# Gated cross-attention with a mixture of experts: half of the projections placed between the score matmuls

## The chip, the core and the metric

The kernel runs on one core of a Trainium2 chip. The metric is the device time of one execution in microseconds (us). The core has TensorE (matmuls into PSUM, which has 8 banks), VectorE, ScalarE, GpSimd (which the code calls pool) and SyncE (sp), whose queue only issues DMAs. Each engine runs its own instructions strictly in the order written, and waits on semaphores for the others.

## What is computed

B = 8 batches of S = 512 tokens with D = 512 channels; attention has 16 heads of 32 channels.

```python
def ref_attention(query, key, value):
    Q, K, V = proj(query, Wq, bq), proj(key, Wk, bk), proj(value, Wv, bv)
    scores = jnp.einsum('bhqd,bhkd->bhqk', Q, K) / SCALE
    attn = jax.nn.softmax(scores, axis=-1)
    out = jnp.einsum('bhqk,bhkd->bhqd', attn, V)
    out = out.transpose(0, 2, 1, 3).reshape(B, S, D)
    return out @ Wo.T + bo
...
x = x + jnp.tanh(g_xattn[0]) * ref_attention(_layernorm(x), ctx_1024, ctx_1024)
x = x + jnp.tanh(g_ffn[0]) * ref_ffn(_layernorm(x))   # 8 experts, top 2, capacity 1.2
```

## The kernel before

**Stages.** Attention comes first, batch by batch, then the routing, then the experts. The change lies in attention alone. Products are kept exact enough by splitting each operand into a high and a low half of 16 bits, so a projection of one 128x512 tile is 12 matmuls: 4 tiles of the contraction, 3 pairs of halves.

**A batch on TensorE** (the function batch under block.tensor). First come the 8 query and key products, qk 0 to 7 in the order q0, k0, q1, k1 and so on (96 matmuls, line 1158). ScalarE copies each out of PSUM twice (qk32 and the high half in qks), GpSimd subtracts for the low half (line 515, "the split"), and SyncE's queue sends both halves to DRAM and back, stacked three high, into stk (stack_heads, one write and three reads for each product). Heads 4m to 4m + 3 need products 2m and 2m + 1.

Then come SLOTS = 23 slots. Slot s has up to four scores matmuls (line 1236), whose only use is the maximum of each row, which VectorE takes from PSUM (line 831, banks 0 and 1 in turn). Every fourth slot the maxima of four heads are split, transposed (mhl, mrow) and sent into row 96 of stk. Six slots later, less_maxima (line 1246) computes the same scores transposed, less the maxima, for unit u = s - 6, in two halves (banks 2, 3 and 4, 5). ScalarE takes their exponentials (line 709, pt), and slot s has with_values and with_ones for unit s - 7 (lines 1255 and 1262), which add up in banks 6 and 7 over the four units of a group. At a group's end ScalarE copies both banks (osum), VectorE takes four reciprocals and multiplies (t32, line 874), ScalarE makes the high half aT (line 721) and GpSimd the low one. Group 1's t32 falls in slot 17, group 2's in slot 20. After the slots TensorE does the output product (48 matmuls, line 1335), banks 2, 4, 0 and 1.

**Between the pairs of scores** lie other pieces: the value product v (48 matmuls, line 1273) in slots 0, 1, 3 and 4 to 5, as halves of six matmuls, and the router of the batch before: transposes of x2n in slot 2, parts and logits in slot 4. In slots 16 to 22 the next batch's normalised x and ctx are transposed, one 128x512 tile in each slot from 16 to 21 and two in slot 22, in banks 1 and 0 in turn (inputs_transposed). VectorE makes their high half (line 807), then their low half (line 810), which frees the bank:

```python
if not (isinstance(b, int) and b == 0):
    ps, _ = filled(dve, act_use, ("actT", n, kt), b)
    v.tensor_scalar(actT[:, n, 0, kt, :], ps, (1.0, SX)[n], None, ALU.mult).then_inc(act_hi, 1)
```

**Order on the other engines** is the order of the code too. In one slot VectorE does: mhl (in every fourth), four maxima, input halves, reciprocals, t32, statistics for the next layer norm (LN_SLOT, slots 6 to 9). ScalarE does: copies of v and of the router, two exponentials, osum, aT. Behind the slots VectorE adds the residual, takes statistics, normalises to x2n with deviations from GpSimd (inverse_deviation), and splits x2n in x2hl.

**Banks.** A class Banks counts the uses of each bank; claim waits on TensorE until the use before has been read, filled waits on a reader until TensorE has written, and copied waits until a use has been read.

Of the kernel before, what the change touches and what calls it, by code (L numbers as in the profile page):

```python
# [45 lines left out]
LN_SLOT = LAG_B  # L46
V_HALF = ((0, 0), (1, 1), (3, 3), (4, 5))
V_SLOT = [last for _, last in V_HALF]
X2T_SLOT, LG_SLOT = 2, 4
GROUP_END = [LAG_C + 4 * g + 3 for g in range(NG)]  # L50
GROUP_NORM = [t + 3 if t < UNITS else min(t + 2, SLOTS) for t in GROUP_END]

# [31 lines left out]
def layer_kernel(nc, x, ctx_in, g_x, g_f, Wq, bq, Wk, bk, Wv, bv, Wo, bo, Wr, br, W1, b1, W2, b2, out):  # L84
# [9 lines left out]
    with stack:  # L94
# [175 lines left out]
        bank_full = [sem(f"bank_full{i}") for i in range(6 + 1)]  # L270
        bank_read = [sem(f"bank_read{i}") for i in range(6 + 1)]
# [103 lines left out]
        def _(sp):  # L375
# [35 lines left out]
            def batch(b, first, last):  # L411
# [12 lines left out]
                for i in range(NQ):  # L424
                    stack_heads(sp, b, i)
                for g in range(NG):
# [5 lines left out]
                    if g == 0:  # L432
                        if not first:
# [47 lines left out]
        def _(pool):  # L481
# [159 lines left out]
        def _(act):  # L641
# [8 lines left out]
            s.activation(bias[:, 8:12], ps[:, 8:12], ACT.Copy, scale=SA).then_inc(bias_ready, 1)  # L650

            def inputs_hi(n, kt):

                ps, _ = filled(act, pre, ("actT", n, kt))
                s.activation(actT[:, n, 0, kt, :], ps, ACT.Copy, scale=(1.0, SX)[n]).then_inc(act_hi, 1)

            for n in range(4):
# [3 lines left out]
                if n < 2:  # L661
                    for kt in range(KT):
                        inputs_hi(n, kt)
            act.wait_ge(bias_ready, 2)

            def router_copy(where, b, slot):
# [6 lines left out]
                def logits():  # L673
                    ps, read = filled(act, where, "lg_parts", b)
                    s.activation(lg_parts[:, :], ps, ACT.Copy).then_inc(read, 1)
                    ps, read = filled(act, where, "lg", b)
# [814 lines left out]
```

## Time and profile before

| | |
|---|---|
| time, median of 3 runs | 1959.96 us (1959.57 to 1960.15) |
| profiled execution, own time | 1961.34 us |
| its span, first to last instruction | 1959.6 us |
| mean granted clock of TensorE | 0.964 |
| busy share of the span: TensorE, VectorE, ScalarE, GpSimd | 91%, 60%, 40%, 25% |
| attention in the span | about 0 to 960 us |
| one batch of it (first scores to first scores) | 402.26 to 519.6 us |
| a middle slot | 3.94 us |

In the profile PE is TensorE, DVE VectorE, ACT ScalarE, POOL GpSimd and SPq the queue of SyncE. An L number is a line of the kernel. A row names what an instruction writes, an arrow, and what it reads; "x6" behind it is a count of instructions merged in the row. The brackets say how long the engine had been idle before it and which engine's instruction ended that. A granted clock of 1.00 is TensorE at full rate.

### The profile page before, as it was taken

What the parts mean: (1) busy time and instruction counts of PE and PEld (TensorE: products, weight loads), DVE (VectorE), ACT (ScalarE), POOL (GpSimd) and SP (SyncE); (2) the same over time, 40 slices, a digit from 0 to 9 for tenths busy, and PEclk for the clock granted to TensorE, in tenths of its full rate; (3) what the DMA queues carried; (4) which work ended last, traced back from release to release, by engine and by line L of the source; (5) the groups of instructions that cost most, each with busy time, mean ns of one, the idle gap of its engine ahead of it and who ended that gap; (6) DMA issues with size and microseconds to landing.
All of it is one profiled execution on the core that took longest, in us unless ns stands there. A gap on an engine that the chain in (4) does not pass through costs nothing.

```text
span 1959.6 us, 30460 instructions
## 1 busy us (share of the span) xinstructions
PE 1788.7 (91%) x10822; PEld 919.9 (47%) x10822; DVE 1167.3 (60%) x2163; ACT 780.9 (40%) x1012; POOL 484.3 (25%) x451
## 2 busy tenths in 40 slices
PE   7999999999999999999811799999999999999996
PEld 4334242332424334242200566667676767666664
DVE  5777868777686777867587453635354443534330
ACT  5443634445354443634430342515161524334240
POOL 2313333232333313331141121221212211112101
PEclk9999999999999999999955899999999999999998
DMA  6214123150322414023130153433334342424311
GB/s 223 84 44 151 45 94 100 48 166 22 127 66 82 133 43 153 19 73 100 37 141 1 48 141 72 149 77 121 102 96 124 82 140 50 154 66 138 70 45 25
DMA packets 138205, 178.97 MB, mean 91 GB/s; under 512 B 45492, under 2 KB 86592, under 8 KB 134056
## 3 DMA queue, kind: packets, MB, share of 16 engines
q1 hardware_dynamic: 97192, 157.85, 24.7%
q0 software_dynamic: 40960, 20.41, 6.0%
q8 instruction: 33, 0.54, 0.1%
q14 instruction: 20, 0.16, 0.0%
HBM read 134.08 MB, written 43.63 MB: 91 GB/s over the span
## 4 chain that ended last, share of the span: by engine, by line
PE 83%; DVE 9%; ACT 3%; issue 2%; DMA 2%; SPq 1%; POOL 1%; DVEq 0%; ACTq 0%; POOLq 0%
PE psum L1445 21%; PE psum L1422 20%; PE psum L1158 7%; PE psum L1255 6%; PE psum L1262 6%; PE psum L1246 5%; PE psum L1236 5%; PE psum L1335 4%; PE psum L1273 4%; DVE mx L831 2%; PE psum L1163 2%; ACT osum L717 1%; DMA qk_rows<-qks 1%; PE psum L1398 1%; DVE cmp L980 1%
## 5 line engine op out<-in xcount | busy, mean ns | idle before, releaser
L1445 PE MATMUL psum<-w,hT 128*123 128x512 f16 x1920 | 420.3, 379 | 0.0
L831 DVE TENSOR_REDUCE mx<-psum 128x1 f32<-128x512 f32 x512 | 328.5, 684 | 153.4 <-PE psum L1236 152.6
L1422 PE MATMUL psum<-xgT,w 128*128 128x308 f16 (+1 forms) x3072 | 411.3, 294 | 0.6 <-DVE xgT L1089 0.6
L1422 PEld LDWEIGHTS psum<-xgT,w 128*128 128x128 f16 x3072 | 298.4, 97 | 109.7 <-DVE xgT L1089 0.8
L1445 PEld LDWEIGHTS psum<-w,hT 128*123 128x123 f16 x1920 | 257.9, 135 | 148.8
L709 ACT ACTIVATE pt<-psum 128x1024 f32<-128x1024 f32 x256 | 259.3, 1022 | 171.0 <-PE psum L1246 171.0
L759 ACT ACTIVATE h<-psum,b1c 128x308 f32<-128x308 f32 (+1 forms) x256 | 118.1, 512 | 379.4 <-PE psum L1422 379.0
L1107 DVE TENSOR_TENSOR hT<-h,hT 128x615 f16<-128x615 f32 x128 | 102.6, 801 | 212.2 <-ACT hT L762 212.1
L629 POOL DMA_INDIRECT out_dram<-y,idx_now x40 | 98.9, 2473 | 499.6 <-DVE y L1142 273.9
L1236 PE MATMUL psum<-stk 96*128 96x512 f16 x512 | 171.7, 384 | 20.0 <-DVE mx L831 18.9
L1158 PE MATMUL psum<-actT,wT 128*128 128x512 f16 x768 | 168.6, 381 | 2.0 <-DVE wT L818 2.0
L743 ACT ACTIVATE w<-stage 128x2048 f16<-128x2048 f32 x64 | 121.7, 1902 | 101.4 <-DMA stage<-in_L_ffn_W_dram 101.4
L1084 DVE SCALAR_TENSOR_TENSOR w<-stage,w 128x512 f16<-128x512 f32 x240 | 156.7, 685 | 0.3 <-issue 0.3
L1246 PE MATMUL psum<-stk 98*128 98x512 f16 x512 | 154.1, 382 | 0.9 <-DMA stk<-mrow 0.9
L1255 PE MATMUL psum<-pt,v 128*32 128x512 f32 x1024 | 137.1, 608 | 5.3 <-ACT osum L717 5.0
L1262 PE MATMUL psum<-pt,ones 128*32 128x512 f32 x1024 | 136.2, 604 | 0.0
L1236 PEld LDWEIGHTS psum<-stk 96*128 96x128 f16 x512 | 43.8, 98 | 192.6 <-DVE mx L831 144.8
L1139 DVE SCALAR_TENSOR_TENSOR y<-psum,b2b 123x512 f32<-123x512 f32 x40 | 27.7, 692 | 178.8 <-PE psum L1445 178.8
L1158 PEld LDWEIGHTS psum<-actT,wT 128*128 128x128 f16 x768 | 75.4, 98 | 93.7 <-issue 4.3
L583 POOL DMA_INDIRECT xg<-x_split,idx_new x40 | 62.0, 1551 | 221.7 <-issue 178.9
L515 POOL TENSOR_TENSOR qks<-qk,qks 128x512 f16<-128x512 f32 x64 | 82.6, 1297 | 76.8 <-ACT qks L692 75.7
L535 POOL TENSOR_SCALAR a<-t,bias 128x512 f32<-128x512 f32 x32 | 22.3, 696 | 315.9 <-DVE t L874 315.9
(181 smaller groups left out, 1682.1 us busy)
## 6 DMA issues: line engine op xcount, KB each, us to landing
stage<-in_L_ffn_W_dram SPq DMA_DIRECT2D x64, 1024.0 KB, 5.0
stk<-qk_rows SPq DMA_DIRECT2D x192, 128.0 KB, 2.5
qk_rows<-qks SPq DMA_DIRECT2D x64, 256.0 KB, 2.6
xin<-in_x_dram SPq DMA_DIRECT2D x8, 1024.0 KB, 5.1
cin<-in_ctx_dram SPq DMA_DIRECT2D x8, 1024.0 KB, 5.1
xres<-in_x_dram SPq DMA_DIRECT2D x8, 1024.0 KB, 5.8
out_dram<-xres SPq DMA_DIRECT2D x32, 256.0 KB, 2.1
x_split<-x2hl SPq DMA_DIRECT2D x32, 256.0 KB, 2.3
```

What stands on the lines that cost most here:

```text
L709: s.activation(pt[:, (2 * u + hf) % 4, :, :], psum[:, bank:bank + 2, :], ACT.Exp, scale=1.0 / (math.sqrt(HD) * SQ * SQ)).then_inc(read, 1)
L743: s.activation(dst, stage[:, i % 2, :], ACT.Copy, scale=SW).then_inc(chunk_hi, 1)
L759: s.activation(h32[:, m % 4, c0:c1], psum[:, (2 * m + ch) % 4, 0:c1 - c0], ACT.Silu, scale=1.0 / (SX * SW), bias=b1c[:, e, m:m + 1]).then_ ...
L831: v.reduce_max(mx[:, KT * t + qt:KT * t + qt + 1], ps, AX.X).then_inc(read, 1)
L1084: v.scalar_tensor_tensor(part[1], stage[:, i % 2, cols], SW, part[0], ALU.mult, ALU.subtract).then_inc(chunk_split, 1)
L1158: last = t_.matmul(dst, lhsT, rhs, start=(i == 0), stop=(i == len(pairs) - 1))
L1236: t_.matmul(dst, stk[0:96, 0, s, qt * P:(qt + 1) * P], stk[0:96, 1, s, :], start=True, stop=True).then_inc(full, 1)
L1246: last = t_.matmul(psum[:, 2 + 2 * hf + j, :], stk[0:98, 1, h, kt * P:(kt + 1) * P], stk[0:98, 0, h, :], start=True, stop=True)
L1255: t_.matmul(psum[32 * j:32 * j + 32, 6, :], v32[:, kt, HD * h:HD * h + HD], pt[:, (2 * u + j // 2) % 4, j % 2, :], start=(kt == 0), stop=( ...
L1262: last = t_.matmul(psum[32 * j:32 * j + 32, 7, :], ones32[:, :], pt[:, (2 * u + j // 2) % 4, j % 2, :], start=(kt == 0), stop=(kt == KT - 1))
L1422: mm = t_.matmul(psum[:, (2 * m + ch) % 4, 0:c1 - c0], w1[:, wp, kt, m * P:(m + 1) * P], xgT[:, xp, kt, c0:c1], start=(kt == 0 and (wp, xp ...
L1445: mm = t_.matmul(psum[0:CP, Y_BANK[c], :], hT[:, hp, k, c * CP:(c + 1) * CP], w2[:, wp, k, :], start=(k == 0 and (hp, wp) == (0, 0)), stop ...
```

## The change

- Only four query and key products and two value tiles are done ahead of the slots. Products 4 to 7 move to slots 0, 1, 3 and 4, value tiles 2 and 3 to slots 5 and 6. Each is cut in two halves of six matmuls, one behind each pair of scores; the transposes of slot 2 are cut likewise. parts stays in slot 4, logits goes to slot 5. Banks 3, 5, 6 and 7 take some of these tiles.
- VectorE takes two maxima ahead of mhl and two behind. Its layer-norm statistics move from slots 6 to 9 to slots 1 to 4.
- The high half of the transposed inputs moves from VectorE to ScalarE, behind the two exponentials of the slot. The low half stays on VectorE, and it waits for the high one.
- GpSimd makes the second layer norm's deviations of the batch before ahead of splits 0 and 2 of the next batch, not at the end of the batch.
- SyncE's queue stacks products 0 to 5, sends the maxima of group 0, stacks 6 and 7, and stores the rows of the batch before behind group 1.

```diff
@@ -43,12 +43,23 @@
 UNITS = 4 * NG
 LAG_B, LAG_C = 6, 7
 SLOTS = UNITS + LAG_C
-LN_SLOT = LAG_B
-V_HALF = ((0, 0), (1, 1), (3, 3), (4, 5))
-V_SLOT = [last for _, last in V_HALF]
-X2T_SLOT, LG_SLOT = 2, 4
+LN_SLOT = 1
+QK_FIRST, QK_SLOT = 4, (0, 1, 3, 4)
+V_FIRST, V_SLOT = 2, (5, 6)
+X2T_SLOT, PARTS_SLOT, LG_SLOT = 2, 4, 5
+STORE_GROUP = 1
 GROUP_END = [LAG_C + 4 * g + 3 for g in range(NG)]
 GROUP_NORM = [t + 3 if t < UNITS else min(t + 2, SLOTS) for t in GROUP_END]
+def later_qk(s):
+    return [QK_FIRST + j for j, slot in enumerate(QK_SLOT) if slot == s]
+def later_v(s):
...
@@ -218,21 +229,25 @@
         pre = banks.close(1)
         def batch_banks(last):
-            for i in range(NQ):
-                banks.add(("qk", i), (2, 4, 0, 1, 0, 1, 2, 4)[i])
+            for i in range(QK_FIRST):
+                banks.add(("qk", i), (2, 4, 0, 1)[i])
+            for tt in range(V_FIRST):
+                banks.add(("v", tt), (3, 5)[tt])
             for s in range(SLOTS):
                 for qt in range(2):
                     if s < UNITS:
                         banks.add(("S", s, qt), qt)
+                for i in later_qk(s):
+                    banks.add(("qk", i), (2, 4, 2, 4)[i - QK_FIRST])
                 if s == X2T_SLOT:
                     for kt in range(KT):
-                        banks.add(("x2T", kt), (2, 4)[kt % 2])
-                for tt in range(KT):
-                    if s == V_HALF[tt][0]:
-                        banks.add(("v", tt), (2, 4, 2, 2)[tt])
+                        banks.add(("x2T", kt), (6, 7, 3, 5)[kt])
+                if s == PARTS_SLOT:
+                    banks.add("lg_parts", 6)
+                for tt in later_v(s):
+                    banks.add(("v", tt), (3, 6)[tt - V_FIRST])
                 if s == LG_SLOT:
-                    banks.add("lg_parts", 4)
-                    banks.add("lg", 4)
+                    banks.add("lg", 7)
                 if not last:
...
@@ -421,7 +436,7 @@
                 sp.wait_ge(norm_done, NG * b)
                 settle(sp)
-                for i in range(NQ):
+                for i in range(QK_FIRST + 2):
...
@@ -430,6 +445,9 @@
                     for a in range(4):
                         sp.dma_start(rows[:, :, a, :], mrow[32 * a:32 * a + 32, g, :]).then_inc(mrow_in[g], 16)
                     if g == 0:
+                        for i in range(QK_FIRST + 2, NQ):
+                            stack_heads(sp, b, i)
+                    if g == STORE_GROUP:
                         if not first:
                             store_rows(b)
...
@@ -504,11 +522,14 @@
             for tt in range(KT):
                 inverse_deviation(0, tt, tt)
-            def batch(b, last):
+            def batch(b, first, last):
                 heads_stacked(pool, b)
                 for i, (which, m) in enumerate(QK_ORDER):
+                    if i in (0, 2) and not first:
+                        for tt in (i, i + 1):
+                            inverse_deviation(1, tt, KT * b + (tt - KT))
                     n = "qk".index(which)
                     pool.wait_ge(qk32_ready, NQ * b + i + 1)
...
-                for tt in range(KT):
-                    inverse_deviation(1, tt, KT * b + tt)
-            batch(0, False)
+            batch(0, True, False)
             with pool.Fori(1, B - 1) as b:
-                batch(b, False)
-            batch(B - 1, True)
+                batch(b, False, False)
+            batch(B - 1, False, True)
+            for tt in range(KT):
+                inverse_deviation(1, tt, KT * (B - 1) + tt)
...
+            s.activation(bias[:, 8:12], ps[:, 8:12], ACT.Copy, scale=SA).then_inc(read, 1)
+            def inputs_hi(b, n, kt):
+                ps, _ = filled(act, act_use, ("actT", n, kt), b)
                 s.activation(actT[:, n, 0, kt, :], ps, ACT.Copy, scale=(1.0, SX)[n]).then_inc(act_hi, 1)
...
                     ps, read = filled(act, where, "lg", b)
                     settle(act)
                     s.activation(lg[:, slot, :], ps[:, 0:KT * E], ACT.Copy).then_inc(read, 1)
-                return rows, logits
+                return rows, parts, logits
             def batch(b, last):
-                rows, logits = router_copy(use, b, b)
-                heads_stacked(act, b)
...
@@ -691,12 +714,25 @@
                                  bias=bias[:, 4 * n + m:4 * n + m + 1]).then_inc(qk32_ready, 1)
                     s.activation(qks[:, n, 0, m, :], ps, ACT.Identity, scale=SQ / (SX * SW),
                                  bias=bias[:, 4 * n + m:4 * n + m + 1]).then_inc(read, 1)
+                def values(tt):
+                    ps, read = filled(act, use, ("v", tt), b)
+                    s.activation(v32[:, tt, :], ps, ACT.Copy, scale=1.0 / (SX * SW)).then_inc(read, 1)
+                heads_stacked(act, b)
+                for i in range(QK_FIRST):
+                    queries_keys(i)
+                for tt in range(V_FIRST):
+                    values(tt)
                 for t in range(SLOTS + 1):
-                    if t in V_SLOT:
-                        ps, read = filled(act, use, ("v", V_SLOT.index(t)), b)
-                        s.activation(v32[:, V_SLOT.index(t), :], ps, ACT.Copy, scale=1.0 / (SX * SW)).then_inc(read, 1)
+                    for i in later_qk(t):
+                        queries_keys(i)
                     if t == X2T_SLOT:
                         rows()
+                    if t == PARTS_SLOT:
+                        parts()
+                    for tt in later_v(t):
+                        values(tt)
                     if t == LG_SLOT:
                         logits()
                     u = t - LAG_B
...
@@ -708,6 +744,9 @@
                             _, read = filled(act, use, ("ST", u, hf), b)
                             s.activation(pt[:, (2 * u + hf) % 4, :, :], psum[:, bank:bank + 2, :], ACT.Exp,
                                          scale=1.0 / (math.sqrt(HD) * SQ * SQ)).then_inc(read, 1)
+                    if not last:
+                        for i in act_tiles(t):
+                            inputs_hi(b + 1, i // KT, i % KT)
                     if t in GROUP_END[:-1]:
                         gr = GROUP_END.index(t)
...
@@ -802,9 +842,6 @@
             def inputs_split(b, n, kt):
-                if not (isinstance(b, int) and b == 0):
-                    ps, _ = filled(dve, act_use, ("actT", n, kt), b)
-                    v.tensor_scalar(actT[:, n, 0, kt, :], ps, (1.0, SX)[n], None, ALU.mult).then_inc(act_hi, 1)
                 dve.wait_ge(act_hi, 2 * KT * b + (KT * n + kt + 1))
                 ps, read = read_by_last(act_use, ("actT", n, kt), b)
                 v.scalar_tensor_tensor(actT[:, n, 1, kt, :], ps, (1.0, SX)[n], actT[:, n, 0, kt, :],
...
@@ -843,6 +880,7 @@
                         v.reciprocal(osum[:, 1, i * P:(i + 1) * P], sums[:, i * P:(i + 1) * P]).then_inc(rinv_done, 1)
                 for t in range(SLOTS + 1):
+                    maxima(t, (0, 1))
                     if t % 4 == 0 and 4 <= t <= UNITS:
                         g = t // 4 - 1
                         for qt in (2, 3):
@@ -856,7 +894,7 @@
                         dve.wait_ge(mrow_in[g], 64 * b)
                         v.transpose(mrow[:, g, :], mhl[:, g, :]).then_inc(mrow_ready, 1)
-                    maxima(t, range(KT))
+                    maxima(t, (2, 3))
                     if not last:
                         for i in act_tiles(t):
                             inputs_split(b + 1, i // KT, i % KT)
...
@@ -1220,14 +1258,22 @@
             def batch(b, last_batch, first=False):
                 rows, parts, logits = router(use, b, KT * b)
-                for i, (which, m) in enumerate(QK_ORDER):
+                def queries_keys(i, halves=range(2)):
+                    which, m = QK_ORDER[i]
                     n = "qk".index(which)
                     if m == 0:
                         for kt in range(KT):
                             copied(pe, act_use, ("actT", n, kt), b)
-                    dst, full = claim(pe, use, ("qk", i), b)
-                    product(dst, [(wT[:, n, wp, kt, m * P:(m + 1) * P], actT[:, n, xp, kt, :])
-                                  for kt in range(KT) for wp, xp in PARTS]).then_inc(full, 1)
+                    if 0 in halves:
+                        claim(pe, use, ("qk", i), b)
+                    bank, _ = use(("qk", i), b)
+                    for kt in [2 * half + j for half in halves for j in range(2)]:
+                        for wp, xp in PARTS:
+                            last = t_.matmul(psum[:, bank, :], wT[:, n, wp, kt, m * P:(m + 1) * P], actT[:, n, xp, kt, :],
+                                             start=(kt == 0 and (wp, xp) == (0, 0)),
+                                             stop=(kt == KT - 1 and (wp, xp) == (1, 0)))
+                    if 1 in halves:
+                        last.then_inc(bank_full[bank], 1)
...
@@ -1263,19 +1309,36 @@
                                              pt[:, (2 * u + j // 2) % 4, j % 2, :], start=(kt == 0), stop=(kt == KT - 1))
                         last.then_inc(pv_done, 1)
-                def values(tt, half):
-                    if half == 0:
+                def values(tt, halves=range(2)):
+                    if 0 in halves:
                         claim(pe, use, ("v", tt), b)
                     bank, _ = use(("v", tt), b)
-                    for kt in (2 * half, 2 * half + 1):
+                    for kt in [2 * half + j for half in halves for j in range(2)]:
                         for xp, wp in PARTS:
                             last = t_.matmul(psum[:, bank, :], actT[:, 1, xp, kt, tt * P:(tt + 1) * P], wT[:, 2, wp, kt, :],
                                              start=(kt == 0 and (xp, wp) == (0, 0)),
                                              stop=(kt == KT - 1 and (xp, wp) == (1, 0)))
-                    if half == 1:
+                    if 1 in halves:
                         last.then_inc(bank_full[bank], 1)
+                def filling(s, half):
+                    for i in later_qk(s):
+                        queries_keys(i, (half,))
+                    if s == X2T_SLOT:
+                        rows((2 * half, 2 * half + 1))
+                    if (s, half) == (PARTS_SLOT, 1):
+                        parts()
+                    for tt in later_v(s):
+                        values(tt, (half,))
+                    if (s, half) == (LG_SLOT, 1):
+                        logits()
+                for i in range(QK_FIRST):
+                    queries_keys(i)
+                for tt in range(V_FIRST):
+                    values(tt)
                 if first:
                     pe.wait_ge(k_ones, 1)
                 for s in range(SLOTS):
...
@@ -1284,14 +1347,12 @@
                         pe.wait_ge(stk_in[s // 4], 96 * b + 96)
                     scores(s, 0)
                     scores(s, 1)
-                    if s == X2T_SLOT:
-                        rows()
-                    for tt in range(KT):
-                        if s in V_HALF[tt]:
-                            values(tt, V_HALF[tt].index(s))
-                    if s == LG_SLOT:
-                        parts()
+                    filling(s, 0)
                     u = s - LAG_B
+                    if u == 0:
+                        copied(pe, use, ("v", 2), b)
+                        copied(pe, use, ("x2T", 3), b)
                     if 0 <= u < UNITS and u % 4 == 0:
                         pe.wait_ge(mrow_in[u // 4], 64 * b + 64)
                     less_maxima(u, 0)
@@ -1306,6 +1367,8 @@
                             if v_ == 0:
                                 pe.wait_ge(norm_done, NG * b)
+                                copied(pe, use, ("v", 3), b)
+                                copied(pe, use, "lg", b)
                             else:
                                 pe.wait_ge(osum_ready, (NG - 1) * b + v_ // 4)
                         for hf in range(2):
@@ -1317,12 +1380,8 @@
                     scores(s, 2)
                     less_maxima(u, 1)
                     scores(s, 3)
-                    for tt in range(KT):
-                        if V_HALF[tt] == (s, s):
-                            values(tt, 1)
-                    if s == LG_SLOT:
-                        logits()
                     with_ones(s - LAG_C)
+                    filling(s, 1)
                 for gs in (range(KT - 1), range(KT - 1, KT)):
                     for tt in range(KT):
                         if gs[0] == 0:
```

## Rows read from the trace of the kernel before

**Rows 1.** TensorE's waits in one batch: who waited for whom, us, times, longest
```profile
PE psum L1236 <- DVE mx L831: 2.4, 6, 0.6
PE psum L1255 <- ACT osum L717: 0.6, 3, 0.3
PE psum L1216 <- ACT t L675: 0.3, 1, 0.3
PE psum L1273 <- ACT v L697: 0.3, 1, 0.3
PE psum L1163 <- ACT x2nT L671: 0.2, 1, 0.2
```

**Rows 2.** Timeline of TensorE, slots 19 and 22: start, us, what
```profile
357.54 0.61 PE L1246 MATMUL psum<-stk 98*128 98x512 f16 x2
...
358.75 1.06 PE L1255 MATMUL psum<-pt,v 128*32 128x512 f32 x8 [0.17 <-ACT osum L717]
...
368.29 1.09 PE L1163 MATMUL psum<-ident,cin 128*128 128x128 f32 x8
```

**Rows 3.** Timeline of ScalarE, slots 17, 18 and 21
```profile
353.20 1.02 ACT L709 ACTIVATE pt<-psum 128x1024 f32<-128x1024 f32 x1 [1.01 <-PE psum L1246]
354.64 0.72 ACT L721 ACTIVATE aT<-t,bias 128x512 f16<-128x512 f32 x1 [0.42 <-DVE t L874]
355.27 1.00 ACT L709 ACTIVATE pt<-psum 128x1024 f32<-128x1024 f32 x1
...
366.83 1.92 ACT L709 ACTIVATE pt<-psum 128x1024 f32<-128x1024 f32 x2
```

**Rows 4.** Timeline of VectorE, slots 17 and 20
```profile
352.33 0.69 DVE L810 SCALAR_TENSOR_TENSOR actT<-psum,actT 128x512 f16<-128x512 f32 x1
352.94 0.94 DVE L843 RECIPROCAL osum<-osum 128x128 f32<-128x128 f32 x1
353.92 0.69 DVE L874 TENSOR_TENSOR t<-osum 128x512 f32<-128x512 f32 x1
...
363.69 1.75 DVE L843 RECIPROCAL osum<-osum 128x128 f32<-128x128 f32 x2
```

**Rows 5.** Timeline of TensorE, projections and slots 0 to 3
```profile
381.54 20.88 PE L1158 MATMUL psum<-actT,wT 128*128 128x512 f16 x96
402.26 0.60 PE L1236 MATMUL psum<-stk 96*128 96x512 f16 x2
...
403.99 0.60 PE L1236 MATMUL psum<-stk 96*128 96x512 f16 x2
...
411.88 0.60 PE L1236 MATMUL psum<-stk 96*128 96x512 f16 x2
413.05 0.39 PE L1236 MATMUL psum<-stk 96*128 96x512 f16 x1 [0.57 <-DVE mx L831]
413.65 0.39 PE L1236 MATMUL psum<-stk 96*128 96x512 f16 x1 [0.21 <-DVE mx L831]
```

**Rows 6.** Timeline of VectorE, slots 2, 6 and 7
```profile
412.30 2.48 DVE L831 TENSOR_REDUCE mx<-psum 128x1 f32<-128x512 f32 x4 [1.42 <-PE psum L1236]
...
427.74 0.69 DVE L785 BATCH_NORM_STATS2 stats<-xin 128x6 f32<-128x512 f32 x1
...
428.68 2.73 DVE L831 TENSOR_REDUCE mx<-psum 128x1 f32<-128x512 f32 x4
```

**Rows 7.** Timeline of VectorE, the end of a batch: casts for x2hl
```profile
388.62 1.38 DVE L894 CAST x2hl<-x2n 128x512 f16<-128x512 f32 x1
...
393.50 0.42 DVE L894 CAST x2hl<-x2n 128x512 f16<-128x512 f32 x1
```

**Rows 8.** Timeline of ScalarE, a copy of v
```profile
306.46 0.60 ACT L697 ACTIVATE v<-psum 128x512 f32<-128x512 f32 x1 [1.38 <-PE psum L1273]
```

**Rows 9.** Timeline of TensorE, the first projections of batch 0
```profile
27.96 22.40 PE L1158 MATMUL psum<-actT,wT 128*128 128x512 f16 x96 [2.00 <-DVE wT L818]
```

**Rows 10.** Busy us by engine, then granted clock, just behind that wait
```profile
28.00:30.00 2.00, 2.00 (x5) 0.65 (x6) 0.59 (x1) 0.00 (x0) 0.00 (x0) 0.50 0.50 111
```

More of the change, by code:

```diff
@@ L45 @@
 SLOTS = UNITS + LAG_C
-LN_SLOT = LAG_B
-V_HALF = ((0, 0), (1, 1), (3, 3), (4, 5))
-V_SLOT = [last for _, last in V_HALF]
-X2T_SLOT, LG_SLOT = 2, 4
+LN_SLOT = 1
[3 more added lines that the diff above has]
+STORE_GROUP = 1
 GROUP_END = [LAG_C + 4 * g + 3 for g in range(NG)]
 GROUP_NORM = [t + 3 if t < UNITS else min(t + 2, SLOTS) for t in GROUP_END]
+def later_qk(s):
+    return [QK_FIRST + j for j, slot in enumerate(QK_SLOT) if slot == s]
+def later_v(s):
+    return [V_FIRST + j for j, slot in enumerate(V_SLOT) if slot == s]
 def act_tiles(s):
@@ L268, in act_use @@
             return pre(key) if isinstance(b, int) and b == 0 else use_loop(key, b, back=1)
-        bank_full = [sem(f"bank_full{i}") for i in range(6 + 1)]
-        bank_read = [sem(f"bank_read{i}") for i in range(6 + 1)]
+        bank_full = [sem(f"bank_full{i}") for i in range(8)]
+        bank_read = [sem(f"bank_read{i}") for i in range(8)]
         def claim(pe, where, key, b=0):
@@ L662, in _ @@
                     for kt in range(KT):
-                        inputs_hi(n, kt)
-            act.wait_ge(bias_ready, 2)
+                        inputs_hi(0, n, kt)
+            act.wait_ge(bias_ready, 1)
+            copied(act, pre, "bias")
             def router_copy(where, b, slot):
@@ L671, in rows, with parts, logits @@
                         s.activation(x2nT[:, kt, :], ps, ACT.Copy).then_inc(read, 1)
-                def logits():
+                def parts():
                     ps, read = filled(act, where, "lg_parts", b)
                     s.activation(lg_parts[:, :], ps, ACT.Copy).then_inc(read, 1)
+                def logits():
                     ps, read = filled(act, where, "lg", b)
@@ L678, in logits, with queries_keys @@
                     s.activation(lg[:, slot, :], ps[:, 0:KT * E], ACT.Copy).then_inc(read, 1)
-                return rows, logits
+                return rows, parts, logits
             def batch(b, last):
-                rows, logits = router_copy(use, b, b)
-                heads_stacked(act, b)
-                for i, (which, m) in enumerate(QK_ORDER):
+                rows, parts, logits = router_copy(use, b, b)
+                def queries_keys(i):
+                    which, m = QK_ORDER[i]
                     n = "qk".index(which)
@@ L726, in _ @@
             batch(B - 1, True)
-            rows, logits = router_copy(post, 0, B)
+            rows, parts, logits = router_copy(post, 0, B)
             rows()
+            parts()
             logits()
@@ L1193, in router, with rows @@
             def router(where, b, n):
-                def rows():
+                def rows(kts=range(KT)):
                     pe.wait_ge(x2n_ready, n)
-                    for kt in range(KT):
+                    for kt in kts:
                         dst, full = claim(pe, where, ("x2T", kt), b)
@@ L1222, in batch @@
                 rows, parts, logits = router(use, b, KT * b)
-                for i, (which, m) in enumerate(QK_ORDER):
+                def queries_keys(i, halves=range(2)):
+                    which, m = QK_ORDER[i]
                     n = "qk".index(which)
@@ L1275, in values @@
                                              stop=(kt == KT - 1 and (xp, wp) == (1, 0)))
-                    if half == 1:
+                    if 1 in halves:
                         last.then_inc(bank_full[bank], 1)
+                def filling(s, half):
[4 more added lines that the diff above has]
+                    if (s, half) == (PARTS_SLOT, 1):
+                        parts()
+                    for tt in later_v(s):
[6 more added lines that the diff above has]
+                    values(tt)
                 if first:
```

3 lines of the change are left out of this document (removed).

## Prediction

> **What bounds the kernel now.** I read the busy shares by stage first: attention takes the first 960 us of the span, about 117.3 us for each of 8 batches, and the change touches nothing behind it. Then the waits of one whole batch, slots 0 to 22 and the products around them [rows 1]: TensorE idles 3.8 us of 117.3, so it is the bound in every slot, and no reordering can give back more than 3.8 x 8 = 30 us, 1.6%. Of the 2.4 us on VectorE, 1.8 lie in the early slots (0.57 and 0.21 behind slot 2, the same behind slot 5, 0.26 behind slot 6) and 0.55 in slot 12. Last I read the timelines of TensorE, VectorE and ScalarE side by side, early and late in the batch, to see which engine is only just on time. That is the larger question: in slots 16 to 22 ScalarE waits for VectorE's t32 and the exponentials behind it are only just early enough [rows 2 to 4].
>
> **Early slots: what the change gives.** A batch's projections are 96 + 48 matmuls at 0.216 us, before and after; nothing is saved but waits. The rhythm: VectorE starts a maximum 0.42 us after its scores (411.88 to 412.30), the next follows 0.62 later (2.48 for 4), and the bank is free 0.75 after the start (413.05, and 413.65 for the second) [rows 5, 6]. Pairs 1.73 us apart (402.26 to 403.99, six matmuls between) never wait. With halves between all pairs the five early waits on VectorE go (1.82), and so do the three on ScalarE's copies (0.3, 0.3, 0.2), as the copied banks now change and parts and logits lie a slot apart: 2.56 us a batch, **-20.5 us** for 8. In slot 12 the first two maxima now go ahead of the mhl operations, 0.49 us earlier, which leaves 0.13 of 0.55: **-3.4 us**.
>
> **What the early part costs.** (a) POOL now makes two of the four inverse deviations only behind splits 0 and 1. VectorE needs them for x2n, and its casts for x2hl (0.42 us alone, 1.38 while GpSimd works on its splits from 388.3 on [rows 7]) end at about 398.5 in place of 396.5. Scores start 24 matmuls earlier, 397.1 in place of 402.3. So the first maxima start 1.0 late, and the next two scores wait 0.42 and 0.38: 0.8 us in 7 batches, **+5.6** (0 if the casts meet no split, 1.9 a batch if all do). (b) The statistics of the next layer norm, 0.94 us each (427.74 to 428.68 [rows 6]), move from slots of 3.94 us to slots 1 to 4 of 3.0 to 3.5, where maxima take 2.5. Walked through pair by pair: waits of 0.14 and 0.40 in slot 2, 0.22 in slot 3, 0.08 in slot 4: 0.84 in 7 batches, **+5.9** (0 to 1.5 a batch). (c) v3 moves to slot 6. Its second half is TensorE's last work of that slot, and ScalarE's in-order queue has its copy ahead of both exponentials of unit 0. Let X be the end of the half: the copy starts X+0.19 and takes 0.60, as now [rows 8]; the exponential starts X+0.70, ends X+1.72, and less_maxima of unit 1, which writes the bank that it reads, starts X+1.78 in place of X+0.43: 1.35. The second exponential ends X+2.64 and with_values starts X+2.70 in place of X+2.31: 0.39. 1.74 us in 8 batches, **+13.9** (0 if the bank were free, 2.6 if nothing overlapped).
>
> The heads' DMA chain shortens with the scores: the two deviations moved let split 0 end at 387.1 in place of 389.7, so that the third stk transfer lands at about 396.5, TensorE arriving at 397.1. I cost it at nothing; without those 0.6 us it is 0 to 1 a batch. SP has mrow of group 0 behind six stackings, ready some 4 us ahead of slot 6. Storing the rows and xres move one group later; xres lands near 447, GpSimd's bias ends at 452, and its first a32 is due at 457: nothing.
>
> The Trainium skill ("SBUF — State Buffer", section Who interferes with whom) says that VectorE's two-port and two-input forms and GpSimd lock each other out for a whole instruction. The cast of 1.38 against 0.42 agrees; by that rule moving splits away from the tail speaks for this change, by the deviations against it, and (a) lies between its bounds above.
>
> **Late slots: what the moved high halves cost.** Now VectorE makes high and low half of each transposed tile as soon as TensorE is done. After, ScalarE makes the high one, behind both exponentials of its slot, and VectorE's low half waits there, ahead of its reciprocals and t32. I walk one batch [rows 2 to 4], slot 17 onwards:
> - exponential (11,1) starts 353.20; the next ScalarE step is 0.92 later, so high half 1 runs 354.12 to 354.72. VectorE's low half starts 354.75 (now 352.33), the reciprocal 0.61 later, t32 0.98 later at 356.34 (353.92), aT 0.72 later at 357.06 (354.64), exponential (12,0) 0.63 later at 357.69 (355.27). It is 2.42 late; it ends 358.71.
> - less_maxima of unit 13 needs its bank: 358.77 in place of 357.54, **1.23**.
> - exponential (12,1) 358.61, high half 2 359.53, osum 360.12 to 361.14 (a 128x1024 copy, 1.02 as an exponential). with_values of unit 12 starts 361.20 in place of 358.75. TensorE is **2.45** late.
> - Slot 20 starts 363.73. Exponential (14,1) 366.40, high half 4 367.32, low half 367.95, two reciprocals 368.56, t32 1.79 later at 370.35, aT 371.07, exponentials 371.70 and 372.62, high half 5 373.54, low half 374.17 to 374.86.
> - Slot 22 has tiles 6 and 7, and tile 7 needs the bank of tile 5. It starts 374.92; due at 368.29 + 0.51 + 2.45 = 371.25. **3.67**.
> Sum 6.12 us. Behind it all moves along: VectorE's four last reciprocals start 5.9 later, TensorE reaches group 3 of the output product 6.1 later. Seven batches have it: **+42.8** (bounds: 0.6 a batch, if only osum were later by a copy; 8 a batch, if t32 waited for each high half in full).
>
> **The clock.** At 28 us TensorE had stood still for 2.00 us, and its granted clock in the 2 us that followed was 0.50, the lower of its levels, 1.2 GHz of 2.4; 96 matmuls took 22.40 us where 20.88 is normal [rows 5, 9, 10]. I take 1.5 us for a fall. The stall of 3.67 in slot 22 is longer: 7 x 1.5 = 10.5. Stalls of 1.23 + 1.22 in slots 18 to 19 and 1.35 + 0.39 in slot 7 are near it: half of 15 x 1.5, 11. **+22** (0 to 33). The Trainium skill ("TensorE: Matmul & The Clock Gate", Part 1) states that an idle array falls to half its clock and must earn it back. The row agrees with that; without such falls the sum would be 22 less.
>
> **The sum.** -20.5 - 3.4 + 5.6 + 5.9 + 13.9 + 42.8 + 22 = +66 us, against the profiled execution's span of 1959.6 and own time of 1961.3. The median shown is 1.4 below that time, so 1960 + 66 = **2026 us**.
>
> **Rivals.**
> - *ScalarE's queue as above, forecast*: 2026, its own range 2004 (clock never falls) to 2045 (falls at every stall, and the stk chain 1 us late). Chance 0.66.
> - *The late stalls are smaller.* Should t32 not wait for low halves, only osum is late, by one copy of 0.6: 4.2 in place of 42.8, and no clock fall there: 1960 + 5.7, with slot 7 falling 0 to 12: 1966 to 1978; half way to the forecast 1990. For it: ScalarE is busy for 40% of the span only. Against it: VectorE's order, low half, reciprocal, t32, is plain [rows 4]. Chance 0.18.
> - *Faster: ScalarE's idle time absorbs v3 and the high halves.* Decisive is whether exponential (12,0) is less than 1.19 us late, the room between its end (356.3) and the 357.54 at which its bank is wanted, and (0,0) likewise. Then -20.5 - 3.4 + 11.5 = -12: 1948. The walk has 2.42 against 1.19. Chance 0.05.
> - *VectorE and the clock worse*: falls cascade, each making the next group's t32 later: above 2045. Chance 0.08.
> - *It does nothing*: the same matmuls, stalls that only change place: 1960. Chance 0.03.
>
> Within 0.2% (4 us) is about what a measurement can't tell from no change. Faster by more: 0.05. Same: 0.03. Slower: 0.92. Leaving out the ends of the rivals: 1990 to 2046.
>
> **What would show it.** In the changed profile: the early waits for mx after slots 2 and 5 gone, a wait of about 1.3 us of the first less_maxima of slot 7, a wait of about 1.2 at slot 19 for ScalarE's pt, then osum 1.2, and one of 3 to 4 us of the transposes of cin for VectorE's actT; t32 of group 2 some 5 us later against the transposes; granted clock below 1.00 in attention windows. I am wrong if ScalarE's exponentials stay 0.65 us behind less_maxima in slots 18 to 21, if the batch is under 119 us, or if the first scores wait for stk.

## The result, and the profile after

| | before | changed |
|---|---|---|
| time, median | 1959.76 us (1958.46 to 1960.15, 4 runs) | 2015.82 us (2011.98 to 2021.84, 4 runs) |
| profiled execution, own time | 1961.34 us | 2011.98 us |
| its span | 1959.6 us | 2010.2 us |
| mean granted clock | 0.964 | 0.958 |

The changed kernel takes 1.0289 times as long, 95% interval 1.0267 to 1.0312. The forecast was 2026 us with 1990 to 2046. The spread of the changed kernel, 10 us, is much wider than the 1.7 us of the kernel before. The clock is the likely cause: the mean granted clock of the four runs was 0.958, 0.957, 0.955 and 0.953 at 2011.98, 2012.99, 2018.64 and 2021.84 us, and 0.005 of 2015 us is 10 us.

TensorE's waits in the changed kernel, over the whole of attention: who waited for whom, us, times, longest. They answer to [rows 1], which are of one batch.

```profile
PE psum L1201 <- DVE actT L847: 24.4, 7, 3.5
PE psum L1292 <- ACT pt L745: 17.3, 15, 1.2
PE psum L1301 <- ACT osum L756: 12.7, 24, 1.3
PE psum L1282 <- DVE mx L868: 11.0, 22, 1.8
...
PE psum L1301 <- ACT pt L745: 3.5, 9, 0.4
```

The kernel before, over its attention:

```profile
PE psum L1236 <- DVE mx L831: 18.9, 48, 0.6
```

Two of the changed kernel's rows did not exist before: the transposes wait for VectorE's low half (7 batches), and less_maxima for an exponential (8 batches in slot 7, 7 in slot 19). with_values waited for an exponential once before, 0.3 us, and now nine times. The waits for the copies x2nT, t and v are gone, and those for mx fell from 18.9 to 11.0 us.

The timeline of TensorE in the batch that begins at 289.21 us. The first three rows are at slot 7, the next at slot 12, then slots 19 and 22; they answer to [rows 2].

```profile
316.81 0.60 PE L1282 MATMUL psum<-stk 96*128 96x512 f16 x2
318.58 0.61 PE L1292 MATMUL psum<-stk 98*128 98x512 f16 x2 [1.17 <-ACT pt L745]
319.59 1.06 PE L1301 MATMUL psum<-pt,v 128*32 128x512 f32 x8 [0.40 <-ACT pt L745]
...
344.48 0.39 PE L1282 MATMUL psum<-stk 96*128 96x512 f16 x1 [1.75 <-DVE mx L868]
...
366.56 1.06 PE L1308 MATMUL psum<-pt,ones 128*32 128x512 f32 x8
368.77 0.60 PE L1292 MATMUL psum<-stk 98*128 98x512 f16 x2 [1.14 <-ACT pt L745]
369.21 0.60 PE L1201 MATMUL psum<-ident,xn 128*128 128x128 f32 x4
371.08 1.40 PE L1301 MATMUL psum<-pt,v 128*32 128x512 f32 x8 [1.27 <-ACT osum L756]
...
382.21 0.66 PE L1201 MATMUL psum<-ident,cin 128*128 128x128 f32 x4
386.35 1.12 PE L1201 MATMUL psum<-ident,cin 128*128 128x128 f32 x4 [3.49 <-DVE actT L847]
```

The reader sees four stalls. Each is priced by start times, as in the prediction. Slot 7: less_maxima was due 0.43 us after the scores at 316.81, at 317.24, and started at 318.58, 1.34 late (forecast 1.35); with_values was due 0.53 behind it and came 0.48 late (0.39). Slot 19: due at 367.56, 1.00 behind with_ones, started 1.21 late (1.23), and then with_values at 371.08 for 369.74, 1.34 late; in the kernel before it was itself 0.24 late there (358.75 for 358.51 in [rows 2]), so 1.10 is new (1.22). Slot 22: tile 7 due 0.51 behind tile 6, at 382.72, started 3.63 late (3.67). Only slot 12 was not forecast.

ScalarE and VectorE in slots 17 to 22 of the same batch, which answer to [rows 3, 4]:

```profile
363.22 1.02 ACT L745 ACTIVATE pt<-psum 128x1024 f32<-128x1024 f32 x1 [1.01 <-PE psum L1292]
364.14 0.59 ACT L675 ACTIVATE actT<-psum 128x512 f16<-128x512 f32 x1
367.08 0.72 ACT L760 ACTIVATE aT<-t,bias 128x512 f16<-128x512 f32 x1 [2.35 <-DVE t L912]
367.71 1.92 ACT L745 ACTIVATE pt<-psum 128x1024 f32<-128x1024 f32 x2
369.52 0.60 ACT L675 ACTIVATE actT<-psum 128x512 f16<-128x512 f32 x1
369.99 1.03 ACT L756 ACTIVATE osum<-psum 128x1024 f32<-128x1024 f32 x1
```

```profile
364.77 0.69 DVE L847 SCALAR_TENSOR_TENSOR actT<-psum,actT 128x512 f16<-128x512 f32 x1 [1.96 <-ACT actT L675]
365.37 0.94 DVE L880 RECIPROCAL osum<-osum 128x128 f32<-128x128 f32 x1
366.35 0.69 DVE L912 TENSOR_TENSOR t<-osum 128x512 f32<-128x512 f32 x1
```

This is the chain of the prediction, link by link: the exponential at 363.22, the high half 0.92 later, the low half that idled 1.96 us for it, the reciprocal, t32 at 366.35, aT at 367.08, and only then the exponential at 367.71, which stands 4.49 us behind the one at 363.22. Before, it was 2.07 (353.20 to 355.27), so it is 2.42 late, the number forecast. ScalarE idled 2.35 us in the middle of it: it was blocked, not busy.

VectorE and GpSimd at slot 12 of the same batch:

```profile
340.01 1.22 DVE L868 TENSOR_REDUCE mx<-psum 128x1 f32<-128x512 f32 x2
341.15 1.23 DVE L889 TENSOR_SCALAR mhl<-mx 128x16 f16<-128x16 f32 x1
342.41 1.19 DVE L891 SCALAR_TENSOR_TENSOR mhl<-mx,mhl 128x16 f16<-128x16 f32 x1
343.64 0.21 DVE L896 STREAM_TRANSPOSE mrow<-mhl 128x32 f16<-128x32 f16 x1
```

```profile
338.61 4.96 POOL L550 TENSOR_TENSOR xres<-xres,tgbo 128x512 f32<-128x512 f32 x4 [16.01 <-DMA xres<-in_x_dram]
```

Two operations on 16 columns take 1.23 and 1.19 us while GpSimd adds the bias to xres, four operations from 338.61 to 343.57.

Granted clock, the number behind the busy times and ahead of DMA share and GB/s, in stretches around slots 19 and 22:

```profile
369.00:371.00 2.00, 0.81 (x6) 0.50 (x4) 0.69 (x1) 2.00 (x4) 0.21 (x1) 1.00 0.00 0
371.00:374.00 3.00, 2.92 (x14) 0.49 (x18) 0.00 (x0) 1.40 (x3) 0.00 (x0) 0.61 0.00 0
385.00:388.00 3.00, 1.65 (x8) 0.92 (x12) 1.29 (x2) 1.56 (x4) 0.00 (x0) 0.56 0.00 0
388.00:391.00 3.00, 3.00 (x17) 0.43 (x10) 0.69 (x1) 0.10 (x1) 0.00 (x0) 0.50 0.37 109
```

### The profile page after: what moved, and what is told of

It reads as the page before. It is cut to its first block, busy times and chain, and to the rows that moved or that the text cites. A ratio compares the mean times of both kernels' runs of the same rounds, so it can differ in the third digit from the quotient of the medians.

```text
span 2010.2 us, 30517 instructions
## 1 busy us (share of the span) xinstructions
PE 1799.2 (90%) x10822; PEld 923.5 (46%) x10822; DVE 1135.3 (56%) x2107; ACT 804.1 (40%) x1068; POOL 474.7 (24%) x451
## 4 chain that ended last, share of the span: by engine, by line
PE 75%; DVE 13%; ACT 5%; issue 4%; POOL 1%; DMA 1%; DVEq 0%; SPq 0%; ACTq 0%; POOLq 0%
PE psum L1504 21%; PE psum L1481 19%; PE psum L1301 6%; PE psum L1308 5%; PE psum L1272 5%; PE psum L1282 5%; PE psum L1292 4%; PE psum L1394 4%; DVE mx L868 3%; PE psum L1319 2%; ACT pt L745 2%; PE psum L1201 1%; ACT osum L756 1%; DVE osum L880 1%; PE psum L1457 1%
## 5 line engine op out<-in xcount | busy, mean ns | idle before, releaser
L1272 PE MATMUL psum<-actT,wT 128*128 128x512 f16 x768 | 177.6, 379 | 2.0 <-DVE wT L855 2.0
L1301 PE MATMUL psum<-pt,v 128*32 128x512 f32 x1024 | 142.2, 628 | 16.2 <-ACT osum L756 12.7
L1308 PE MATMUL psum<-pt,ones 128*32 128x512 f32 x1024 | 141.7, 626 | 0.0
L536 POOL TENSOR_TENSOR qks<-qk,qks 128x512 f16<-128x512 f32 x64 | 75.3, 1176 | 196.4 <-ACT qks L715 196.4
L713 ACT ACTIVATE qk<-psum,bias 128x512 f32<-128x512 f32 x64 | 44.0, 688 | 181.8 <-PE psum L1272 176.5
```

Of the source, the lines that this page charges most:

```text
L1272: last = t_.matmul(psum[:, bank, :], wT[:, n, wp, kt, m * P:(m + 1) * P], actT[:, n, xp, kt, :], start=(kt == 0 and (wp, xp) == (0, 0)), s ...
L1301: t_.matmul(psum[32 * j:32 * j + 32, 6, :], v32[:, kt, HD * h:HD * h + HD], pt[:, (2 * u + j // 2) % 4, j % 2, :], start=(kt == 0), stop=( ...
L1308: last = t_.matmul(psum[32 * j:32 * j + 32, 7, :], ones32[:, :], pt[:, (2 * u + j // 2) % 4, j % 2, :], start=(kt == 0), stop=(kt == KT - 1))
```

## Experiments

Times are medians. The first four ran beside a median before of 1958.31 us, the next four beside 1959.56, the last four beside 1959.44; a difference to the 2015.82 of the changed kernel is between runs on different occasions, and holds to about 1.5 us beside that kernel's own spread.

**1. High halves back on VectorE.** The changed kernel with

```diff
-                    if not last:
-                        for i in act_tiles(t):
-                            inputs_hi(b + 1, i // KT, i % KT)
...
             def inputs_split(b, n, kt):
+                if not (isinstance(b, int) and b == 0):
+                    ps, _ = filled(dve, act_use, ("actT", n, kt), b)
+                    v.tensor_scalar(actT[:, n, 0, kt, :], ps, (1.0, SX)[n], None, ALU.mult).then_inc(act_hi, 1)
```

> The changed kernel with the high halves of the inputs made by VectorE again, everything else as changed. Theory (ScalarE's queue): the waits of slots 19 and 22 go, 1.14 + 1.10 + 3.49 us in 7 batches = 40 us, and with them the falls of the clock behind them, some 8 us more: about 1968 us (1960 to 1975). Rival (the loss is made in the early slots, by v3, the statistics and the heads' transfers): it stays above 1995 us.

Measured: 1961.24 us, ratio to before 1.0017 (1.0006 to 1.0028). That is 54.6 us less than the 2015.82 of the changed kernel. The stalls of slots 19 and 22 are gone; the early ones stand:

```profile
PE psum L1282 <- DVE mx L868: 11.9, 22, 1.8
...
PE psum L1292 <- ACT pt L745: 9.4, 8, 1.2
```

The theory holds, and the rival, that the early part makes the loss, falls.

**2. v3 behind the exponentials.** In ScalarE's loop:

```diff
-                    for tt in later_v(t):
-                        values(tt)
+                    if t < LAG_B:
+                        for tt in later_v(t):
+                            values(tt)
...
+                    if t >= LAG_B:
+                        for tt in later_v(t):
+                            values(tt)
```

> The changed kernel with ScalarE's copy of v3 behind the two exponentials of unit 0, not ahead of them. Theory: the waits of 1.17 and 0.40 us in slot 7 go in 8 batches, 12.6 us: about 2003 us, and since no fall of the clock was seen behind that stall, hardly more. Rival (the exponentials were late for another reason, v3 is free): 2016 us, and with_values waits for v3 instead.

Measured: 1998.11 us (1989.75 to 2003.43), 17.7 less. The timeline of TensorE at the end of slot 6 and in slot 7:

```profile
322.60 0.60 PE L1286 MATMUL psum<-stk 96*128 96x512 f16 x2
323.04 0.60 PE L1296 MATMUL psum<-stk 98*128 98x512 f16 x2
323.56 1.07 PE L1305 MATMUL psum<-pt,v 128*32 128x512 f32 x8
```

No wait is left; with_values doesn't wait for the copy of v3 either. By start times the stall was 1.34 + 0.48 us in 8 batches, 14.6 us; the rest of the 17.7 lies within the spread of this kernel.

**3. Rows stored and xres loaded behind group 0**, one constant, STORE_GROUP = 0.

> The changed kernel with the rows stored and xres loaded behind group 0, as before, so that GpSimd adds the bias to xres some 10 us earlier. Theory (port shared by GpSimd and VectorE): GpSimd's bias work of 5 us no longer meets VectorE's mhl operations of slot 12, which fall from about 1.2 us each to 0.2, and the wait of 0.7 to 1.75 us there goes: 8 us, about 2007 us. Rival (the mhl operations are slow by themselves where they stand now, behind the first maxima): the wait stays and the time is 2015 us.

Measured: 2010.11 us, 5.7 less. VectorE at slot 12:

```profile
348.00 0.16 DVE L889 TENSOR_SCALAR mhl<-mx 128x16 f16<-128x16 f32 x1
348.20 0.18 DVE L891 SCALAR_TENSOR_TENSOR mhl<-mx,mhl 128x16 f16<-128x16 f32 x1
```

GpSimd's bias work now began at 335.88, 12 us ahead of these rows. TensorE's waits for mx fell from 11.0 to 2.9 us. So the position behind the first maxima is not slow; the meeting with GpSimd is. The time fell by less than the 8.1 us of waits, and the clock fell more often in this run's trace, at slot 19 in 4 of 7 batches against 1 of 7 and at slot 22 in 7 against 5. Its mean is 0.954 against 0.958, by estimate 8 us of the span if TensorE were busy throughout, so that part of the gain is not seen.

**4. High halves on ScalarE, between the exponentials.**

```diff
                     for hf in range(2):
                         if 0 <= u < UNITS:
...
+                        if hf == 0 and not last:
+                            for i in act_tiles(t):
+                                inputs_hi(b + 1, i // KT, i % KT)
-                    if not last:
-                        for i in act_tiles(t):
-                            inputs_hi(b + 1, i // KT, i % KT)
```

> The changed kernel with the high halves still on ScalarE, but between the two exponentials of their slot, not behind both. Theory (place in the queue, not load): ScalarE is free there for about 1.1 us and the copy needs 0.6, so that the low halves start only 0.4 us later than before; the 40 us of late waits shrink to at most 5, and the clock falls with them: about 1972 us (1963 to 1985). Rival (ScalarE is too busy for 8 more copies a batch): above 2000 us.

Measured: 1965.31 us, 50.5 less than the changed kernel, with the same work on the same engine. ScalarE in slot 17:

```profile
354.13 1.02 ACT L745 ACTIVATE pt<-psum 128x1024 f32<-128x1024 f32 x1 [0.45 <-PE psum L1292]
355.05 0.59 ACT L675 ACTIVATE actT<-psum 128x512 f16<-128x512 f32 x1
356.16 1.02 ACT L745 ACTIVATE pt<-psum 128x1024 f32<-128x1024 f32 x1 [0.52 <-PE psum L1292]
```

The copy lies wholly in idle time; 0.52 us are left behind it. The loss was the place in the queue, not ScalarE's load. A wait of 0.54 to 0.60 us for tile 5's low half is left in 7 batches, and osum is some 0.3 later in slot 19.

**5. The kernel before with the high halves on ScalarE** behind both exponentials, and nothing else of the change.

```diff
-                    v.tensor_scalar(actT[:, n, 0, kt, :], ps, (1.0, SX)[n], None, ALU.mult).then_inc(act_hi, 1)
...
+                    if not last:
+                        for i in act_tiles(t):
+                            inputs_hi(b + 1, i // KT, i % KT)
```

> The kernel before with one part of the change alone: the high halves of the inputs on ScalarE, behind both exponentials. Theory: the whole late loss is there without anything of the early slots, 1.14 + 1.10 + 3.49 us in 7 batches = 40 us of waits and some 10 us of falls of the clock: about 2010 us. Rival (the loss needs the early parts too): below 1980 us.

Measured: 2022.29 us, ratio 1.0320 (1.0303 to 1.0337). The part alone costs 62.7 us, more than the whole change. Its waits are the forecast's (the first 960 us, which leave out the last slots of batch 7):

```profile
PE psum L1163 <- DVE actT L810: 24.4, 7, 3.5
PE psum L1236 <- DVE mx L831: 18.2, 46, 0.6
PE psum L1255 <- ACT osum L720: 11.8, 21, 1.3
...
PE psum L1246 <- ACT pt L709: 7.9, 7, 1.1
```

The expectation was 12 us low, and some 10 of them are the clock: the granted clock fell behind the stall of slot 22 in all 7 batches, each time for some 7 us, as in the row below, against 5 of 7 in the changed kernel, two of them only 3 us long. From slot 7 to slot 7 six of its batches take 126.1 to 126.3 us for 117.4 before; 6.0 of that are the late stalls, so each fall costs 2.8 us, 20 in 7 batches for the 10 expected. The rest of the 12 us are idle times that are too short (below).

```profile
646.00:653.00 7.00, 6.99 (x28) 2.29 (x29) 3.48 (x5) 0.60 (x1) 0.00 (x0) 0.56 0.46 150
```

**6 and 7. Three mends.** The edits of experiments 2 and 3 together, with the high halves as in experiment 4 (6) or as in experiment 1 (7).

> The changed kernel with three mends: v3 behind the exponentials, rows stored behind group 0, high halves on ScalarE between the exponentials. Theory (the waits add up singly): 1965 - 12.6 - 8 = 1944 us, faster than before by 0.7%. Rival (the waits only change place, one mend's gain is eaten by the next wait): above 1955 us.

> As the run with three mends, but with the high halves on VectorE. Theory: 1961 - 12.6 - 8 = 1940 us, 4 us below the one with ScalarE's halves, which keeps a wait of 0.5 us for tile 7 and 0.3 for osum in each of 7 batches. Rival: ScalarE's copies free VectorE for the early maxima of the next slots, and the other one is faster.

Measured: 1937.74 us (ratio 0.9895, 0.9878 to 0.9911) and 1932.80 us (0.9868, 0.9852 to 0.9885). Both beat the kernel before, by 1.1 and 1.3%, and both came out 6 to 7 us below the expectation. The waits add up singly, as the theory says; the expectation took their idle times, which are too short (below), and in these two traces no fall of the clock is left in any slot, against three behind slot 12 in experiment 1 and one behind slot 7 in experiment 4. The two differ by 4.9 us, expected 4.

**8. Experiment 6 with the statistics in slots 6 to 9** (LN_SLOT = 6).

> The run with three mends (high halves on ScalarE) and the layer norm's statistics of the next batch back in slots 6 to 9. Prediction's step (b): the early maxima wait 0.84 us less in each of 7 batches, about 6 us faster than that run. Rival: the waits in the early slots are VectorE's late end of the batch before, not the statistics, and the time is the same within 1 us.

Measured: 1932.51 us, 5.2 less than experiment 6.

**9. Experiment 7 with the statistics in slots 6 to 9.**

> Three mends with the high halves on VectorE, and the statistics back in slots 6 to 9. If the statistics cost early maxima 0.84 us in each of 7 batches, 6 us faster than the same kernel with early statistics, about 1927 us. If VectorE, which now has the high halves too, isn't short in slots 1 to 4, the same within 1 us.

**10. Experiment 7 with the deviations ahead of split 0:**

```diff
-                    if i in (0, 2) and not first:
-                        for tt in (i, i + 1):
+                    if i == 0 and not first:
+                        for tt in range(KT):
                             inverse_deviation(1, tt, KT * b + (tt - KT))
```

> Three mends with the high halves on VectorE, and all four deviations of the second layer norm ahead of split 0, as before the change. Prediction's step (a): VectorE ends its batch up to 1 us earlier and the first maxima wait 0.8 us less, up to 5 us faster; but split 0 ends up to 2.6 us later, and the first scores of a batch may wait for stk: up to 2 us in 7 batches, 14 us slower. The prediction's chain had 0.6 us of room there, so it says 7 x (2.0 - 0.8) = 8 us slower.

**11. Experiment 7 with mhl ahead of all four maxima:**

```diff
-                    maxima(t, (0, 1))
...
-                    maxima(t, (2, 3))
+                    maxima(t, range(KT))
```

> Three mends with the high halves on VectorE, and mhl again ahead of all four maxima of its slot. Prediction's step: the wait of 0.55 us in slot 12 comes back in place of about 0.1, in 8 batches 3.4 us slower than the same kernel. Rival: nothing, as the wait moves behind the first pair instead.

**12. Experiment 7 again**, as the base of these three.

> The kernel with three mends and the high halves on VectorE once more, unchanged, as the base for the other runs of this call on the same chip: 1933 us (1928 to 1936).

Measured: 1931.45 us (1931.17 to 1932.61) for the base. Experiment 9: 1925.56 us, 5.9 less, ratio to before 0.9827 (0.9814 to 0.9840); it is the fastest kernel here, 1.7% below the one before, and no wait for mx is left in it. Experiment 10: 1940.65 us, 9.2 more. Experiment 11: 1936.45 us, 5.0 more. The waits of TensorE in experiment 10, and one of the seven in its timeline:

```profile
PE psum L1286 <- DMA stk<-qk_rows: 9.7, 7, 1.6
```

```profile
275.14 0.60 PE L1286 MATMUL psum<-stk 96*128 96x512 f16 x2 [1.30 <-DMA stk<-qk_rows]
```

With the deviations first, the first scores of seven batches wait for the heads' last transfer, 1.2 to 1.56 us. With the order of the change nothing waits there, as the prediction had it, and the new order of GpSimd is a part of the change that pays; how much room is left there no run shows. In experiment 11 the wait of slot 12 is back in all 8 batches, 0.55 or 0.56 us by the timeline, as the kernel before has it:

```profile
450.26 0.39 PE L1236 MATMUL psum<-stk 96*128 96x512 f16 x1 [0.56 <-DVE mx L831]
```

## Why the prediction was right, step by step

- **The late slots, +42.8.** Measured from one with_ones to the next, in batches without a fall of the clock there: slots 18 to 19 took 6.05 us for 3.74 before, slots 21 to 22 6.61 for 2.90, so 6.02 us in 7 batches, 42.1. Shown by experiments 1, 4 and 5: the stalls come with the part alone, are gone with the copy back on VectorE, and shrink to 1.0 us a batch when the copy moves by one place in ScalarE's queue. The rival of an idle ScalarE that absorbs the copies had the right fact and the wrong conclusion: ScalarE idled 2.35 us in this very chain.
- **v3 in slot 7, +13.9.** Measured 1.34 + 0.48 in 8 batches, 14.6; experiment 2.
- **The early gain, -20.5.** Mis-sized. I added the idle times of [rows 1], and those are too short, by a piece that depends on the matmul before. In [rows 5] the scores at 411.88 take two steps of 0.216, so the next were due at 412.31 and came at 413.05, 0.74 late; the row says 0.57 of idle, as it counts from the modelled end of the matmul before, some 0.17 behind the moment at which the next could start (only 0.06 behind with_values: the wait of slot 12, 0.56 by its row, costs 0.62). Priced by start times the eight early waits cost 3.8 us a batch, not 2.56, and one more is too short for the list (the pair of scores at 426.72 took 0.90 us for the usual 0.60): 4.1 us, so the gain was near 33 us. Experiment 9, which has it all and of the costs only (a), is 33.9 us faster than the kernel before; 3.3 of that is slot 12. The prediction's ceiling, that no reordering can give back more than 30 us, was the sum of the same idle times, and this run passes it.
- **Slot 12, -3.4.** Right for the order, wrong in sign for the changed kernel. From with_ones of slot 11 to that of slot 13 the kernel before takes 8.50 us in each batch. Without GpSimd in the way the new order takes 8.09 (experiments 7, 9 and 12), 0.41 less, 3.3 us in 8 batches. That order alone pays 5.0 us in experiment 11, as a smaller wait of slot 4, which the prediction had not looked at, goes with it (first scores to first with_ones 30.52 us for 30.93). In the changed kernel the waits of slot 12 grew instead, to between 0.69 and 1.75 us in 7 batches (9.12 to 11.62 us from with_ones to with_ones; less some 1.5 for each of two falls of the clock, that is 11.9 us in 8 batches over two slots of 3.94, for 5.0 before: +7), because of the step that I costed at nothing: rows stored and xres loaded one group later. I asked only whether the bias was done when its result was due, and it was; not what VectorE does in the 5 us in which GpSimd now works. Experiment 3 shows it: with the bias 12 us ahead, slots 11 to 13 take 8.09 or 8.10 us in 7 of 8 batches. The rule on the shared port of the Trainium skill ("SBUF — State Buffer", section Who interferes with whom), which I applied to the casts, covers this too: both mhl operations are of the kinds that it names. These rows agree with it, 0.16 and 0.18 us alone against 1.23 and 1.19.
- **(a), +5.6.** Too high. In this trace VectorE's first maxima started at 290.11 for 289.63, 0.48 late and not 1.0, and the next two scores took 0.90 us for the usual 0.60: 0.3 us lost. That the deviations' order pays more than it costs (experiment 10) was in the text as the chain's room, but sized at 0 to 1 us a batch, where the old order makes TensorE wait 1.2 to 1.56.
- **(b), +5.9.** Measured 5.2 and 5.9 (experiments 8 and 9).
- **The clock, +22.** Too dear. In stretches of 1 us the attention of the changed kernel has 8 falls: five of 7 behind slot 22, of 3 or 7 us, one behind slot 19, two behind slot 12, none behind slot 7. The kernel before has two, at 27 and 898 us. By the mean granted clock, TensorE would lack 0.036 of 1959.6 us before and 0.042 of 2010.2 now if it were busy throughout: an estimate of 14 us more. The sum agrees: of the 50.6 us by which the span grew, the terms above make some 39 (-33 + 7 + 2 + 6 + 14.6 + 42.1), which leaves 12. No run isolates it.

The forecast was +66 for a measured +56 by the medians and +51 by the profiled execution, which had the highest clock of the four runs. That the total came so close is in part luck. Against the profiled execution an early gain 13 too small, a clock 8 to 10 too dear and (a) 3 too dear pushed it up, and slot 12 pulled it down by 10. What decided the sign was the walk through the late slots, right to 0.1 us a batch.

## What to carry to other kernels

Work moved to an idle engine costs what its place in that engine's order costs, not its duration: follow the moved instruction's result through every queue until it meets the bound engine, and try the neighbouring place; here one place was worth 50 us. Price a stall by start times against the rhythm around it, not by the idle column. When a piece is shifted on an engine off the path, ask what it now overlaps with as well as when it is due.

## What the runs showed of the hardware

- After a wait of 1.99 to 2.00 us at the start, the clock fell in the kernel before (0.50 granted) and not in the changed one, whose trace has 1.00 at 28 to 31 us. Over the traces of the changed kernel and experiments 2, 3 and 5, stalls of 3.49 us let it fall in 25 of 28 cases (5 of 7 and 7 of 7 in the changed kernel and experiment 5). Those of 1.47 to 1.80 at slot 12 did in 5 of 12, over the changed kernel and experiments 1, 2 and 4. Each fall lasts 3 or 7 us: one of 3 cost 1.5 us (22.40 for 20.88 in [rows 5, 9]), one of 7 cost 2.8 (experiment 5). So a price for a fall is an average over chances. The Trainium skill ("TensorE: Matmul & The Clock Gate", Part 1) says of the rise of the clock at a kernel's start that it varies from run to run of the same kernel; these runs show the same of its falls.
- VectorE's operations on 16 columns, out of SBUF, are stretched about seven times by a GpSimd operation on 512 (0.16 to 1.23 us, 0.18 to 1.19), while two maxima out of PSUM beside them take 1.22 us as ever.
